# Second attention of a decoder layer: scores and values in halves of two PSUM banks, projections between the halves

## What is computed

```python
def _L0_xattn_ref(q, k, v, Wq, bq, Wk, bk, Wv, bv, Wo, bo):
    B, S, D, H = (4, 1024, 512, 16)
    HD = D // H
    Q = (q @ Wq.T + bq).reshape(bs, sl, H, HD)
    K = (k @ Wk.T + bk).reshape(bs, sl, H, HD)
    V = (v @ Wv.T + bv).reshape(bs, sl, H, HD)
    score = jnp.einsum('bshd,bsgd->bshg', Q, K)
    weight = jax.nn.softmax(score, axis=-1)
    attn = jnp.einsum('bshg,bsgd->bshd', weight, V).reshape(bs, sl, nf)
    return attn @ Wo.T + bo
...
x = _layernorm(x + _L0_attn_ref(x, ...))
x = _layernorm(x + _L0_xattn_ref(x, ctx_2048, ctx_2048, ...))
x = _layernorm(x + _L0_ffn_ref(x, ...))
```

## Time and profile before

| | us |
|---|---|
| median of 3 runs | 1901.7 |
| lowest, highest | 1899.28, 1902.15 |
| the profiled execution | 1899.83 |
| its span | 1897.9 |
| second attention in it, first score to last turned row | about 350 to 617 |

### The profile page before, as it was taken

The page is one execution under the profiler, slowest core; times in us unless marked ns, Lnnn a source line. Parts: engine busy times, 40 slices in busy tenths (PEclk is TensorE's granted clock), DMA queues, the critical chain, the costliest instruction groups (busy, mean ns, idle before and its releaser), DMA issues.

```text
span 1897.9 us, 37020 instructions
## 1 busy us (share of the span) xinstructions
PE 1763.2 (93%) x14528; PEld 1448.6 (76%) x14528; DVE 1238.2 (65%) x1943; ACT 710.4 (37%) x1492; POOL 266.2 (14%) x237
## 2 busy tenths in 40 slices
PE   4888877799996999999999999999999999999997
PEld 3777765688885777878888888888888888888886
DVE  3667764668775556676676675665756766756776
ACT  4454542212121435353343343433433433434331
POOL 1444542534332000000000000000000000000000
PEclk8889988899998899999999999999999999999999
DMA  4111220100000203012020030020120200300011
GB/s 153 52 38 47 61 66 17 63 13 11 22 0 1 95 1 84 22 54 57 14 80 21 7 93 7 14 85 8 42 56 13 78 21 7 93 7 13 7 50 45
DMA packets 51082, 76.65 MB, mean 40 GB/s; under 512 B 9152, under 2 KB 27712, under 8 KB 50240
## 3 DMA queue, kind: packets, MB, share of 16 engines
q1 hardware_dynamic: 51008, 75.62, 13.3%
HBM read 68.78 MB, written 6.82 MB: 40 GB/s over the span
## 4 chain that ended last, share of the span: by engine, by line
PE 63%; DVE 2%; issue 2%; ACT 1%; POOLq 0%; POOL 0%; DVEq 0%
PE pair L1849 9%; PE pair L1850 9%; PE pair L1851 9%; PE y_ps L1849 3%; PE y_ps L1851 3%; PE y_ps L1850 3%; PE qa_ps L1849 3%; PE qa_ps L1851 3%; PE qa_ps L1850 3%; PE pair L1986 2%; PE pair L1977 2%; PE pair L1976 1%; PE pair L1985 1%; PE qd_ps L2053 1%; PE qd_ps L2054 1%
## 5 line engine op out<-in xcount | busy, mean ns | idle before, releaser
L1849 PE MATMUL pair<-XH,GUH 128*128 128x512 f32 x800 | 313.4, 392 | 0.0
L1850 PE MATMUL pair<-XL,GUH 128*128 128x512 f32 x800 | 312.3, 390 | 0.0
L1851 PE MATMUL pair<-XH,GUL 128*128 128x512 f32 x800 | 312.3, 390 | 0.0
L1849 PEld LDWEIGHTS pair<-XH,GUH 128*128 128x128 f32 x800 | 150.5, 188 | 32.3
L1851 PEld LDWEIGHTS pair<-XH,GUL 128*128 128x128 f32 x800 | 150.4, 188 | 32.2
L1850 PEld LDWEIGHTS pair<-XL,GUH 128*128 128x128 f32 x800 | 150.5, 188 | 31.6
L1413 POOL TENSOR_TENSOR qb_raw<-qb_raw,qb_scale 128x704 f32<-128x704 f32 x8 | 13.6, 1704 | 1057.7 <-DVE G L1567 923.4
L372 ACT ACTIVATE p<-scores_ps,nm 128x128 f32<-128x128 f32 (+1 forms) x256 | 104.1, 433 | 103.2 <-DVE nm L457 103.2
L1763 DVE TENSOR_TENSOR h<-pair,sg 128x512 f32<-128x512 f32 x80 | 55.2, 690 | 131.9 <-ACT sg L1512 130.2
L1423 ACT ACTIVATE HH<-h 128x512 fp32r<-128x512 f32 (+1 forms) x120 | 75.9, 633 | 170.5 <-DVE h L1768 94.0
L1567 DVE TENSOR_TENSOR HL<-h,HH 128x512 fp32r<-128x512 f32 (+1 forms) x120 | 83.4, 695 | 83.9 <-ACT HH L1423 83.9
(11 more groups left out here) (337 smaller groups left out, 4186.5 us busy)
## 6 DMA issues: line engine op xcount, KB each, us to landing
gu_raw<-in_gu SPq DMA_DIRECT2D x20, 512.0 KB, 3.8
wrep<-soft_f SPq DMA_DIRECT2D x64, 128.0 KB
dw_raw<-in_dw SPq DMA_DIRECT2D x10, 512.0 KB, 4.6
xT_raw<-in_xT SPq DMA_DIRECT2D x8, 512.0 KB, 4.1
x_raw<-in_x SPq DMA_DIRECT2D x8, 512.0 KB, 3.7
VR<-v_rows SPq DMA_DIRECT2D x32, 128.0 KB, 2.6
out<-xtok SPq DMA_DIRECT2D x4, 1024.0 KB, 4.3
gu_raw<-in_gu SPq DMA_DIRECT2D x10, 384.0 KB, 3.1
```

What stands on the lines that cost most here:

```text
L1849: mm(out, wh, xh, start=first, stop=False)
L1850: mm(out, wh, xl, start=False, stop=False)
L1851: return mm(out, wl, xh, start=False, stop=last)
```

## The change

`scores(b)` becomes `scores(b, 0)` and `scores(b, 1)`, of two banks each, and `values(b)` likewise. `project(b+1, 0)` stands between the halves of the scores, and `project(b+1, 4)` between those of the values, where it follows `turn_rows(b-1, 0)`. `s_done` counts two in a batch, and `less_maxima(b, w)` waits for its own half; the transposes of keys and queries wait for both. `values(b, 0)` waits only for the first half of PB. `o_done` comes with the second half of the values. Within a half of the scores the four row groups go to two banks, where they went to four.

```diff
@@ keys_turned, queries_turned
-                after(dve, s_done, b)
+                after(dve, s_done, 2 * b)
@@ less_maxima
-                dve.wait_ge(s_done, b + 1)
+                dve.wait_ge(s_done, 2 * b + w + 1)
@@ scores
-            def scores(b):
-                after(pe, sub_rdy, 2 * b)
-                for k in range(4):
+            def scores(b, w):
+                after(pe, sub_rdy, 2 * (b - 1) + w + 1)
+                for k in (2 * w, 2 * w + 1):
...
-                    for n in range(4):
+                    for n in range(2):
                         for g in range(4):
-                            k, rows = (n + g) % 4, slice(32 * g, 32 * g + 32)
+                            k, rows = 2 * w + (n + g) % 2, slice(32 * g, 32 * g + 32)
@@ values
-            def values(b):
-                pe.wait_ge(vt_rdy, b + 1)
-                after(pe, ol_rdy, 2 * b)
-                pe.wait_ge(pb_rdy, 2 * (b + 1))
+            def values(b, w):
+                if w == 0:
+                    pe.wait_ge(vt_rdy, b + 1)
+                    after(pe, ol_rdy, 2 * b)
+                pe.wait_ge(pb_rdy, 2 * b + w + 1)
...
-                for k in range(4):
+                for k in (2 * w, 2 * w + 1):
...
-                done.then_inc(o_done, 1)
+                if w == 1:
+                    done.then_inc(o_done, 1)
@@ batch
-                scores(b)
+                scores(b, 0)
                 if not last:
-                    for n in range(4):
+                    project(b + 1, 0)
+                scores(b, 1)
+                if not last:
+                    for n in range(1, 4):
                         project(b + 1, n)
-                values(b)
+                values(b, 0)
                 if not first:
                     turn_rows(b - 1, 0)
                 if not last:
                     project(b + 1, 4)
+                values(b, 1)
                 if not first:
                     turn_rows(b - 1, 1)
```

More of the change, by code:

```diff
@@ L1080, in project @@
                 done.then_inc(proj_done, 1)
-            def scores(b):
-                after(pe, sub_rdy, 2 * b)
-                for k in range(4):
+            def scores(b, w):
+                after(pe, sub_rdy, 2 * (b - 1) + w + 1)
+                for k in (2 * w, 2 * w + 1):
                     mm(so_ps[:, k, 0:S], identR[:], apart[:].rearrange("p m u h -> p (m u h)"), start=True, stop=False,
                        skip_group_check=True)
-                pe.wait_ge(kb_rdy, 2 * (b + 1))
-                pe.wait_ge(qb_rdy, 2 * (b + 1))
+                if w == 0:
+                    pe.wait_ge(kb_rdy, 2 * (b + 1))
+                    pe.wait_ge(qb_rdy, 2 * (b + 1))
                 alone(pe, past)
                 for m in range(8):
-                    for n in range(4):
+                    for n in range(2):
                         for g in range(4):
-                            k, rows = (n + g) % 4, slice(32 * g, 32 * g + 32)
+                            k, rows = 2 * w + (n + g) % 2, slice(32 * g, 32 * g + 32)
                             done = mm(so_ps[rows, k, 32 * m:32 * m + 32], TQ[rows, :, :, 8 * k + m].rearrange("p s h -> p (s h)"),
```

## The result

The changed kernel takes 1921.4 us (median of 4 runs, 1918.16 to 1924.32), the kernel before in the same rounds 1901.3: a ratio of 1.0107 (95% interval 1.0087 to 1.0127), 20 us slower. The forecast was 1911.1, slower by 9.4; the time is just above the end of its range, 1921.0. The sign and the places were right, the size was half of what came.

A forecast was written before the change was run, and what follows sets the result against it. TensorE, busy 93% of the span, was taken as the bound. Middle batches +17.6, batch 0 +0.4, batch 7 -3.4, pauses -4.1, clock -1.1 sum to +9.4 us: 1911.1 us on the median of 1901.7, range 1905.5 to 1921.

The forecast's parts named there:

- the clock behind the new waits: TensorE's clock after the added waits in middle batches: the sum had no term for a fall there.
- the first wait: Batches 1 to 6: the first turn of rows waits 0.7 us on TensorE for VectorE's first norm.
- the changes of shape: TensorE, each middle batch: four more changes of matmul shape at about 0.1 us, 0.4 us a batch.
- Only TensorE's list counts in the middle batches: Batches 1 to 6: TensorE waits for nothing, so only less work on it or a new wait moves the time.
- The second wait: Batches 1 to 6: the second turn of rows waits 1.84 us for ScalarE's copy, queued behind two attention-output copies.
- Batch 0, the pauses in batches 0 and 1: Batch 0 pays shape changes alone, +0.4 us; four issue pauses in batches 0 and 1 vanish, -4.1 us with batch 7's two.
- The clock of batch 1: Projection behind batch 1's scores: without the pause the clock stays up, -1.1 us, bounds 0 and -2.2.
- Batch 7: Last batch: values need only half the probabilities, shortening the 10.81 us wait; output projection starts 3.4 us earlier.
- rival 2: Middle batches: the clock falls behind each new wait, 1.1 us six times, +6.6 on top of +9.4, 1918 us; chance 0.13.
- Rival 3: Scores: row groups in one bank take turns, up to 3.8 us more in each of eight batches, +30, 1941 us; chance 0.05.

The follow-up runs named there:

- the turns hidden: Changed kernel with each turn of the rows put behind the projection that it stood ahead of: 1896.1 us, ratio 0.9969 to the kernel before.
- The experiment on ScalarE's list: Changed kernel with the copy of the first turned rows moved ahead of the two attention-output copies: 1904.3 us, ratio 1.0007 to the kernel before.
- the last version: Changed kernel with masks first, projections between halves in batch 0 only, turns where they were before, batch 7's last between output projections: 1893.6 us, ratio 0.9951.

## Why the prediction was right in its sign and short in its size

The step that failed is the clock behind the new waits: the sum has no term for it, and the runs showed 1.53 us for each of four falls, 6.1 of the 10.7 us between +9.4 and the measured +20.1. Next to it the first wait was taken at 0.7 us and measured 1.25, 3.3 us over six batches, and the changes of shape at 0.4 and measured 0.68, 1.7 us.

Its steps, in its own order:

- *Only TensorE's list counts in the middle batches.* Right: each wait moved the time by its full length.
- *Changes of shape, 0.4 us a batch.* Mis-sized: 0.68 with the turns hidden, 0.35 with the scores alone in halves. The count of four left out that the mask is written in two pieces as well: they take 0.33 us each (499.88 to 500.21 in batch 4), the whole took 0.56. Over six batches, 1.7 us. That the rest is changes of shape is not shown by itself.
- *The first wait, 0.7 us.* The mechanism was right, and the step that failed in it is "the end of the first norm at 565.12 + 0.92". The earlier trace rows merges two norms in one row of 1.84 us, and I took half for each. The first takes 1.38 and the second 0.53, since GpSimd biases keys during the first. That makes the wait longer by 0.46. The second maximum started 7.63 us into the batch and not 7.45, and VectorE's way from there to the norm took 0.13 longer than before. Against that, the turn itself stands at 18.02 and not 17.75, by the mis-sized changes of shape. With 0.05 from VectorE to TensorE, which the forecast left out, 0.7 + 0.46 + 0.18 + 0.13 + 0.05 - 0.27 = 1.25. Six times 0.55: 3.3 us.
- *The second wait, 1.84 us.* Right: 1.85, and 1.77 in batches 6 and 7. The experiment on ScalarE's list settles that the order of the copies forces it.
- *Batch 0, the pauses in batches 0 and 1.* Right: all four gone, -1.8 us in batch 0 as forecast. Halves without a projection between them (the last version) had pauses of 1.23 and 0.74 us in batch 1, so it is the projection between that takes them away.
- *The clock of batch 1, -1.1.* The fall after the scores did go, but another came behind the second wait.
- *Batch 7, -3.4.* -4.0, in part by luck. Up to the output projection it is -3.6, and 0.5 of that is a pause in the scores of 0.63 and not 1.15 us. The other 0.4 lies in the last two turns of rows, where the clock fell one turn later than in the profile of before; the second profile of that kernel has 39.55 us for the batch instead of 40.44.
- *The clock behind the new waits.* The sum put it at nothing. This was rival 2, at a chance of 0.13 and a price of 1.1 us a fall, and it is the largest part of the miss: 1.53 us in each of four batches, 6.1 us. It was half right: not behind every wait, and dearer. I weighed each idle time against single pauses of before (1.10 us without a fall). The two new waits come within one batch and add up to 3.1 us, and the table above says that among like batches the sum tells better than the longest. The price was short too, since I took it from the earlier trace rows. The low level lasted as long there, from about 391.5 to 394.8 us, but 1 us of it lay over score matmuls, which kept their pace (94 in 392.46 - 390.95 = 1.51 us, 16 ns each). In batch 4 of the change it lay from 528.0 to 531.4, all of it over the projection.
- *Rival 3, row groups in one bank* (the prediction calls it the second where it names the rule). Fallen. The page "TensorEngine Tiling (Array Packing)" of the Trainium skill (Restrictions and Gotchas) says that different row tiles cannot access one bank at the same time; the scores of the last version take 3.87 us either way, so here, in different partitions of the bank, they did not take turns. The measurement decides.

Together: 14.7 forecast for batches 2 to 6 against 23.4 measured is 4.6 for three falls, 2.8 for the first wait and 1.3 for the shapes and small shifts. Batch 1 adds 2.0 of the same kinds; batch 7 gives 0.6 back. From 9.4 that leads to 19.6, the 20 that was measured.

What stays open is what exactly lets the clock fall in one batch and not in the next with the same waits. The runs show only that, behind these waits, falls are more frequent with more idle time in the batch, and vary between executions.

## What to carry to other kernels

Where an engine is busy without a gap, cutting its blocks in pieces brings nothing to it and moves each later step closer to what it depends on. Ask for every step behind the cut which engine's list it waits for and what stands ahead there: moving one copy ahead of two others was worth 18 us here, 11 of them the waits and 6 the clock. Put a long independent piece between a result and its user, and cut only where the engine does wait (here the first and the last batch). And never halve a merged row: ask for the instructions one by one.

## What the runs showed of the hardware

- The same VectorE instruction, 128x512 from SBUF to SBUF, took 1.38 us where a GpSimd instruction of 1.05 us on two SBUF operands began 0.04 us behind it, and 0.53 to 0.55 us where GpSimd stood idle or began only in its last 0.2 us. GpSimd's 1.05 us were the same beside the norm and beside VectorE's transposes.
- The granted clock reached its lower level behind idle times of 1.85 to 3.6 us a batch in 0 to 6 of six batches, in the main the more often the longer; a fall made a batch 1.4 to 1.6 us longer. 94 small score matmuls, two thirds of them at the lower level, kept their 16 ns each.
- The first attention, with the same code, ended between 338.0 and 345.1 us in twelve profiles, with a granted clock of 0.89 to 0.84 in its stretch. A difference of 3 us between two profiles means nothing before it is placed in a stage.
- 128 small matmuls in a row ran without a pause in batches 0 and 1 where 256 had pauses of 0.7 to 1.5 us (beside the one at the very start of batch 0's scores, which stays). In the loop's later passes, batches 2 to 6, 256 had none. Why is not shown.
